# Attention with its work ordered by a build-time model of tasks, and its weighted values in fp32 column halves

## What is computed

```python
x = x + 0.5 * ffn(layernorm(x))                     # experts, top 2 of 8
q = (x @ Wq) -> 16 heads of 64, * 64 ** -0.5        # on layernorm(x)
k, v = split(x @ Wkv)                               # one head each
sim = q @ k.T + rel_bias * 64 ** 0.5; causal mask
x = x + softmax(sim) @ v @ Wout + bout
x = x + 0.5 * ffn(layernorm(x))
```

## Time and profile before

| | |
|---|---|
| median of 3 runs | 1348.94 us (1347.59 to 1349.1) |
| the profiled execution | 1347.8 us, of which the span is 1346.0 us |
| mean granted clock of PE | 0.937 |
| PE, weight loads | busy 1029.9 us (77%), 899.3 (67%) |
| DVE, ACT, POOL | busy 840.0 us (62%), 722.3 (54%), 650.5 (48%) |
| instructions | 23815 |

### The profile page before, as it was taken

One profiled execution on the slowest core, in us unless ns is written; L12 is line 12 of the kernel. 1 busy time (PEld: TensorE's weight loads), 2 busy tenths in 40 slices (PEclk: granted clock), 3 DMA queues, 4 the chain that ended last, 5 costly groups with the idle time before them and its releaser, 6 DMA issues.

```text
span 1346.0 us, 23815 instructions
## 1 busy us (share of the span) xinstructions
PE 1029.9 (77%) x7084; PEld 899.3 (67%) x7084; DVE 840.0 (62%) x2514; ACT 722.3 (54%) x1804; POOL 650.5 (48%) x473
## 2 busy tenths in 40 slices
PE   1428788750899999999999999999999706878870
PEld 1427777740787778878778778877887606777770
DVE  4662222227888887888888888888887493222226
ACT  1102222211888888888889889888898201222220
POOL 1146777743353444434444444444444044777772
PEclk9988999985999999999999999999999658999995
DMA  7896555541000000000000000000000203555545
GB/s 207 116 167 197 147 152 156 151 132 54 1 2 1 1 1 1 2 1 1 1 1 1 1 1 1 1 1 1 1 1 1 63 0 115 154 149 153 152 111 187
DMA packets 61065, 87.13 MB, mean 65 GB/s; under 512 B 8019, under 2 KB 32598, under 8 KB 60944
## 3 DMA queue, kind: packets, MB, share of 16 engines
q1 hardware_dynamic: 51200, 66.08, 18.9%
q0 software_dynamic: 9744, 19.56, 4.9%
HBM read 65.67 MB, written 20.97 MB: 64 GB/s over the span
## 4 chain that ended last, share of the span: by engine, by line
PE 47%; DVE 22%; DMA 10%; issue 9%; POOL 9%; ACT 1%; DVEq 1%; another core or an unknown queue 0%; SPq 0%; POOLq 0%; ACTq 0%
PE bank L1046 8%; DMA xr<-xn_dram,gidx 7%; PE bank L1020 6%; DVE qst L857 6%; PE bank L1036 6%; PE bank L1037 5%; POOL y_dram L504 5%; PE bank L1058 4%; PE bank L1056 4%; DVE prob L879 3%; PE bank L976 3%; POOL xr L498 3%; PE bank L986 3%; DVE x_sb L824 2%; DVE in_tile L753 2%
## 5 line engine op out<-in xcount | busy, mean ns | idle before, releaser
L536 POOL TENSOR_TENSOR prob<-prob,rsum 128x512 f32<-128x512 f32 (+3 forms) x128 | 296.1, 2321 | 381.5 <-DVE rsum L886 381.5
L600 ACT ACTIVATE prob<-prob,negmax 128x384 f32<-128x384 f32 (+3 forms) x512 | 283.2, 556 | 25.9 <-DVE negmax L879 24.2
L879 DVE CUSTOM_DVE_ANT_0 prob<-bank,bias_tab 128x384 f32<-128x384 f32 (+3 forms) x512 | 243.1, 489 | 70.8 <-PE bank L1037 60.2
L578 ACT ACTIVATE hT<-bank 128x512 f32<-128x512 f32 x144 | 86.0, 597 | 372.6 <-PE bank L976 372.6
L891 DVE TENSOR_TENSOR pl<-bank,ph 128x512 fp32r<-128x512 f32 x320 | 219.9, 687 | 26.0 <-ACT ph L609 22.4
L1036 PE MATMUL bank<-kst,qst 128*128 128x256 f32 (+2 forms) x512 | 182.6, 371 | 23.3 <-DVE qst L857 21.0
L609 ACT ACTIVATE ph<-bank 128x512 fp32r<-128x512 f32 x320 | 188.8, 590 | 19.6 <-PE bank L1046 17.3
L1046 PE MATMUL bank<-ident,prob 128*128 128x128 f32 x1280 | 193.7, 274 | 0.7 <-POOL prob L536 0.6
L1046 PEld LDWEIGHTS bank<-ident,prob 128*128 128x128 f32 x1280 | 156.8, 140 | 48.1 <-POOL prob L536 10.2
L815 DVE COPY yo<-bank 128x128 f32<-128x128 f32 x144 | 42.0, 292 | 214.1 <-PE bank L986 209.9
L498 POOL DMA_INDIRECT xr<-xn_dram,gidx x144 | 140.1, 973 | 72.8 <-issue 31.1
(11 more groups left out here) (152 smaller groups left out, 1366.9 us busy)
## 6 DMA issues: line engine op xcount, KB each, us to landing
w1t<-L_ffn_fc_w SPq DMA_DIRECT2D x144, 256.0 KB
in_tile<-y_dram SPq DMA_DIRECT2D x16, 512.0 KB, 4.3
bias_dram<-hg SPq DMA_DIRECT2D x1, 5120.0 KB, 52.9
xn_dram<-in_tile SPq DMA_DIRECT2D x8, 512.0 KB, 2.9
bias_tab<-bias_dram SPq DMA_DIRECT2D x1, 4096.0 KB, 13.0
xr<-xn_dram,gidx POOLq DMA_INDIRECT x144
y_dram<-yo,sidx POOLq DMA_INDIRECT x144
x_sb<-L_attn_x SPq DMA_DIRECT2D x4, 512.0 KB, 7.9
```

The source lines that it names most:

```text
L536: g.tensor_tensor(out=pv, in0=pv, in1=rsum[:, n % 4, :].unsqueeze(2).to_broadcast([P, HG, (n % QT + 1) * P]), op=ALU.mult).then_inc(norm_d ...
L600: a.activation(prob[n % QT][:, h, :], prob[n % QT][:, h, :], ACT.Exp, scale=-1.0, bias=negmax[:, (HG * n + h) % 8:(HG * n + h) % 8 + 1], a ...
L879: v.tensor_tensor_reduce(out=prob[n % QT][:, h, :], in0=front[:, 0:w], in1=bias_tab[:, HG * (n // QT) + h, SEQ - w:SEQ], scale=-1.0, scala ...
```

## The change

Task by task:

- Values are kept in fp32 (`vst`, one ACT copy `VC`, no subtraction). A transposed block is copied once, in fp32, to a ring `pT` of eight blocks, by ACT or by DVE, as the model had it.
- The weighted values of a unit are one task of 2(t + 1) fp32 matmuls of 256 columns with 64 stationary columns: for each block, heads 0 and 2 go to partitions 0 to 63 of the bank, heads 1 and 3 to partitions 64 to 127.
- The copy `ot` has 256 columns, and the output projection two fp32 matmuls that each take two heads at once, with Wout's rows laid out for that and not twice.
- `xTh`, `xTl`, `kst`, `vst` are doubled, `prob` goes from four buffers to eight, `lsum` and `rsum` too.
- The order is made by `attention_order`: it takes all tasks of all batches with a duration, what they need, and which kind of bank they take and free, and plays them through: an engine that is free takes, of the tasks that are ready, the one with the smallest `wanted_at`. Banks are given out in that play, no longer in turn. Semaphore values are counted from the resulting orders.
- The expert stages are the same code.

The core of the diff:

```diff
-RING = 3
+RING = 8
+GROUP = QT * (QT + 1) // 2
+PERIOD = NG * GROUP + 2
+LEAD = 0.7
 S_FIX = 1.1
+HOP = {"same": 0.12, "other": 0.07, "pe": 0.22}
...
-        wo_sb = sb("wo_sb", [P, H, D])
+        wo_sb = sb("wo_sb", [P, NG, 2, D])
...
-            vst = ab("vst", [P, QT, 2 * DH], F32R)
+            vst = ab("vst", [P, 2, QT, DH])
...
-            prob = [ab(f"prob{t}", [P, HG, (t + 1) * P]) for t in range(QT)]
+            prob = [ab(f"prob{n}", [P, HG, (n % QT + 1) * P]) for n in range(8)]
...
-            ph = ab("ph", [P, RING, HG * P], F32R)
-            pl = ab("pl", [P, RING, HG * P], F32R)
-            ot = ab("ot", [P, 2, HG * P])
+            pT = ab("pT", [P, RING, HG * P])
+            ot = ab("ot", [P, 2, 2 * P])
...
+        def attention_tasks():
...
+                    for jj in range(t + 1):
+                        task(("T", b, n, jj), {"pe": 0.44}, [("N", b, n)], "turned")
+                        task(("TC", b, n, jj), {"act": 0.48, "dve": 0.6}, [("T", b, n, jj), ("AV", *ring_user(b, n, jj))],
+                             None, ("T", b, n, jj))
+                    task(("AV", b, n), {"pe": 0.47 * (t + 1) + 0.2}, [("TC", b, n, jj) for jj in range(t + 1)] +
+                         ([("VC", b)] if n == 0 else []) + [("YA", *earlier(b, n, 2))])
...
+        def attention_order():
...
+            while left:
+                for e in order:
+                    if busy[e] > now:
+                        continue
+                    can = [k for k, when in ready[e].items() if when <= now and
+                           (tasks[k][2] is None or any(x[0] <= now for x in free[tasks[k][2]]))]
+                    if not can:
+                        continue
+                    k = min(can, key=wanted_at)
...
+                    order[e].append(k)
+                    left -= 1
+                    busy[e] = now + cost[e]
...
-                        a.activation(ph[:, i % RING, :], PT_BANK[i % 3][:], ACT.Copy).then_inc(ph_done, 1)
+                        a.activation(pT[:, (b * NB + blk(n, jj)) % RING, :], BANK_OF["T", b, n, jj][:], ACT.Copy).then_inc(pt_act, 1)
...
-                        v.tensor_tensor(pl[:, i % RING, :], PT_BANK[i % 3][:], ph[:, i % RING, :].bitcast(F32),
-                                        ALU.subtract).then_inc(pl_done, 1)
+                        v.tensor_copy(pT[:, (b * NB + blk(n, jj)) % RING, :], BANK_OF["T", b, n, jj][:]).then_inc(pt_dve, 1)
...
-                        t_.matmul(OT_BANK[n % 2][:], vst[:, jj, :], ph[:, i % RING, :], start=(jj == 0), stop=False)
-                        pe.wait_ge(pl_done, b * NB + (i + 1))
-                        t_.matmul(OT_BANK[n % 2][:], vst[:, jj, :], pl[:, i % RING, :], start=False, stop=(jj == n % QT)).then_inc(av_ps, 1)
+                        for jj in range(n % QT + 1):
+                            for o in range(2):
+                                heads = pT[:, (b * NB + blk(n, jj)) % RING, :].rearrange("p (c o q) -> p o c q", c=2, o=2)[:, o, :, :]
+                                ins = t_.matmul(BACK_BANK[n % 2][o * DH:(o + 1) * DH, 0:2 * P], vst[:, b % 2, jj, :], heads,
+                                                start=(jj == 0), stop=(jj == n % QT))
+                        ins.then_inc(av_ps, 1)
...
-                        for h in range(HG):
-                            ins = t_.matmul(OT_BANK[n % 2][:, 0:D], ot[:, n % 2, h * P:(h + 1) * P], wo_sb[:, HG * (n // QT) + h, :],
-                                            start=(h == 0), stop=(h == HG - 1))
+                        for c in range(2):
+                            ins = t_.matmul(BACK_BANK[n % 2][:, 2 * P:2 * P + D], ot[:, n % 2, c * P:(c + 1) * P], wo_sb[:, n // QT, c, :],
+                                            start=(c == 0), stop=(c == 1))
```

More of the change, by code:

```diff
@@ L252, in on @@
             return 0 <= k - lag < ETILES
[L254 to L284, removed]
-                a, z = g * group - LEAD + (K_GAP if g == 0 else 0), (g + 1) * group - LEAD
-                for t in range(QT):
-                    for h in range(HG):
-                        done = sum(weight[:t]) + weight[t] * (h + 0.5) / HG
-                        lead(a + (z - a) * done / sum(weight), ("S", 0, g * QT + t, h))
-                    lead(a + (z - a) * sum(weight[:t + 1]) / sum(weight) + LAG_R, ("R", 0, g * QT + t))
-            return sorted(plan, key=lambda x: x[0])
@@ L364, in attention @@
-        def attention(eng, run):
-            run(FIRST, 0)
-            for b in range(BATCH - 1):
-                run(PLAN, b)
-            run(FINAL, BATCH - 1)
+        BACK_BANK = [bank[5], bank[6]]
+        FREE_BANKS = {"front": [bank[0], bank[1], bank[7]], "turned": [bank[2], bank[3], bank[4]]}
         def blk(n, jj):
@@ new lines, in build, with counted @@
+        ORDER, BANK_OF, TAKEN_FROM = attention_order()
+        def counted(engine, kinds, each=1):
+            out, total = {}, 0
+            for k in ORDER[engine]:
+                if k[0] in kinds:
+                    total += each(k) if callable(each) else each
+                    out[k] = total
+            return out
+        MISC_PS, S_PS, PT_PS = counted("pe", ("xT", "K", "V", "Q")), counted("pe", ("S",)), counted("pe", ("T",))
+        AV_PS, PROJ_PS = counted("pe", ("AV",)), counted("pe", ("Y",))
@@ new lines, in build, with freed, in_order @@
+        PLACE = {k: i for e in ORDER for i, k in enumerate(ORDER[e])}
+        def freed(k):
+            if k[0] == "TC":
+                return (pt_act, PT_ACT[k]) if k in PT_ACT else (pt_dve, PT_DVE[k])
+            return {"TTR": (s_done, S_DONE), "VC": (v_done, V_DONE)}.get(k[0], (misc_free, MISC_FREE))[0], \
+                {"TTR": S_DONE, "VC": V_DONE}.get(k[0], MISC_FREE)[k]
+        def in_order(first, second):
+            assert first[1] < 0 or PLACE[first] < PLACE[second], (first, second)
@@ new lines, in build @@
+        for k in ORDER["pe"]:
+            if k[0] == "S":
+                in_order(("T", *earlier(k[1], k[2], 8), k[2] % QT), k)
+            if k[0] == "xT":
+                for reader in (("K", k[1] - 2), ("V", k[1] - 2), ("Q", k[1] - 2, NG - 1, 1)):
+                    in_order(reader, k)
+            if k[0] == "K":
+                for h in range(HG):
+                    in_order(("S", k[1] - 2, NU - 1, h), k)
+            if k[0] == "V":
+                in_order(("AV", k[1] - 2, NU - 1), k)
+            if k[0] == "Q":
+                b2, g2 = (k[1], k[2] - 2) if k[2] >= 2 else (k[1] - 1, k[2] - 2 + NG)
+                for h in range(HG):
+                    in_order(("S", b2, g2 * QT + QT - 1, h), k)
@@ L376, in _ @@
+        for k in ORDER["dve"]:
+            if k[0] == "TTR":
+                in_order(("R", *earlier(k[1], k[2], 8)), k)
         @block.sync
```

475 lines of the change are left out of this document (257 added, 218 removed).

## The result

The changed kernel takes 1259.9 us (median of 4 runs; 1257.9 to 1260.6) against 1348.3 for the kernel before, measured beside it: ratio 0.934, 95% interval 0.932 to 0.935. That is 88 us less, where 64 were forecast.

What follows compares the result with a forecast made beforehand. PE bounds attention with 78.5 us work and 10.0 slack a batch. 78.5 - 7.1 + 2.7 = 74.1, plus 6.5 slack gives 80.6; 7.9 less x 8.12 = 64 us saved, so 1285 us, range 1240 to 1340.

Steps and rivals of the forecast that it cites:

- output projection, 8 passes to 4: Attention, PE: four fp32 matmuls per unit become two, 14.1 to 7.0 us, 7.1 us less a batch.
- a block of values, overlapping: Attention, PE: both column halves' passes run side by side, 0.44 us a block; values cost 2.7 us more a batch overall.
- one pass alone at each unit's end: Attention, PE: halves overlap in turn, so each of 16 units ends with one unpaired pass of 0.22 us.
- rival 2: Attention, PE: going in and out of column halves drains the array, 5.2 us a batch, period 85.8, 1327 us; chance 0.16.
- slack kept: Attention, PE: of 10.0 us slack a batch, about two thirds, 6.5, stays because ACT and DVE get lighter.
- period: Attention, one batch: 80.6 us, which is 7.9 less than before.
- Rival 1: Attention values: column halves run one after the other, period 94.7, 1399 us, or 1428 at the old slack; chance 0.12.
- Rival 3: Attention: fixed order misjudges the chip, late copies hold PE, 1350 to 1365 us, half of it 1320; chance 0.07 beyond 1340.
- Buffers, "they only take waits away": Attention: doubled projection buffers, eight probability buffers and a ring of eight add no instruction; no separate size given.
- values block to block: Sign in PE's timeline of attention: weighted values start 0.44 to 0.5 us from one block to the next.
- bias adds: Sign on POOL in attention: batch-opening bias adds stand 78 to 84 us apart.
- ACT, DVE and the query's wait: Signs in attention: ACT and DVE busy near 63 us a period; PE's waits behind the query's subtraction below 4.7 a batch.

Runs made afterwards that it cites:

- the tuned model: Kernel with values of two neighbouring units together, its order model's durations of scores, projections and values set to traced starts: 1264.7 us, ratio 0.938 to before.
- block by block: Changed kernel with one task of weighted values per block instead of per unit, entering the halves 39.5 times a batch: 1391.7 us on a slower chip, ratio 0.974.
- two units together: Changed kernel with weighted values of two neighbouring units directly behind one another, 8 entries a batch: 1326.8 us on a slower chip, 1254.6 again, ratio 0.929 both.
- old order: Before's order and buffers with the changed kernel's arithmetic (single fp32 copies, column halves block by block, two-matmul projection): 1372.2 us, ratio 1.017 to before.

## Why the prediction came out as it did

The direction, the stage and the bound were right, the measured time lies in the range (1240 to 1340), and 88 us against 64 forecast is a difference of three terms, of which two went one way and the third the other. Per batch:

| step of the prediction | forecast | measured |
|---|---|---|
| output projection, 8 passes to 4 | -7.1 | four passes at 0.11, -7.1 |
| a block of values, overlapping | 0.44 us | 0.43, couples 7 ns apart |
| one pass alone at each unit's end | 3.5 us | none |
| going in and out of halves (rival 2) | 0 in the forecast, 5.2 in the rival | 4.8 (at 0.30) to 5.6 (at 0.35) |
| slack kept | 6.5 of 10.0 | 1.8 |
| period | 80.6 | 77.4 |

74.1 - 3.5 - 0.3 + 5.3 + 1.8 = 77.4. And 3.2 us a batch x 8.12 = 26 us is what separates 1285 from 1260. That the time lies in the range is in part luck: with the pass alone and the slack as measured and nothing for the halves, the sum would have been a period of 72.1 and some 1216 us, under the range's 1240. An unbooked cost of 5.3 us stood against 8.5 us that were booked too high.

*The step that was mis-sized is the slack.* "I keep about two thirds, 6.5, because ACT and DVE go from 74 to 76 of 88 us to about 63 of 80": the reason held only in part. With that relief and before's order the slack stays at 8.3 to 9.5; with the new order and no relief it is 5.9; with both 1.8. So the relief is worth at most 1.7 under the old order and 4.1 under the new one, and the order 4.1 without the relief and 6.5 or more with it: each is worth more where the other is there. The sign was in the earlier trace rows: nearly half of the slack had one cause, a query projection written into the order where its bank is not yet free. That wait stays at 5.6 us a batch with a lighter DVE and is gone with the new order and a full one. I treated a wait that had a name as a share of load.

*The pass left alone* came from the assumption that the halves start in turn. They start in couples; the trace shows this for all 48 units of three batches.

*Rival 2, the cost of going in and out*, came, in the size that it had (0.16 us each way from the length of a transpose less its distance; measured 0.30 to 0.35 for both ways). Whether the array is emptied in that time, as it said, no row shows; the rows show the weight loads that start late. I gave it 0.16 of the chances and left it out of the sum; it should have been in the sum, as a term with a lower bound of 0, and the time of 1327 it gave was wrong because the slack fell and no pass was left alone (4.7 and 3.5 us a batch). The argument I had against it, the change from fp32 to fp32r that costs nothing net, is true and says nothing about halves. My argument for the overlap, that a weight load runs under a matmul, holds inside a group; at its edges the trace shows that it doesn't, and there the price is paid. The Trainium skill, TensorEngine Tiling (Array Packing), Key Properties, says that a change of tiling mode drains TensorE; the traces agree that such a change costs time, with 0.33 us a unit, and show nothing of a drain itself. The Trainium skill's 2.38 times for three column tiles (TensorE: Matmul & The Clock Gate, Part 3, Measured speedup vs the span model) would be 79% of full overlap, an estimate from the page; here two tiles reach all of it inside a unit (0.43 us against 0.86 without halves), and (0.43 x 40) / (0.43 x 40 + 5.3) = 76% with the entries counted.

*Rival 1, halves in sequence*, did not come; what it would have been is near the kernel without halves, whose 87.4 us of work (88.2 in the rival) gave a period of 90.5.

*Rival 3, a misjudged order*, did not come for this order, but the tuned model shows that it can: 2 us a batch from changes in durations of 1 to 3% for scores and projections and of 22% for the projection of the values, with the query's wait back in the trace.

*Buffers, "they only take waits away"*: right, and there was almost nothing to take: 0 for the probabilities, 5 us for the projections. The ring of eight was not tried against one of three.

*The signs that were named*: values block to block took 0.43 us where 0.44 to 0.5 was given, and the bias adds stand 77.4 us apart where 78 to 84 was given, both just outside; ACT, DVE and the query's wait came as given.

What stays open: which of the moves in the new order take which waits, apart from the query's; what the ring has in it; and which of the better durations put the query's projection back where it waits.

## What to carry to other kernels

Split the slack of the bound engine by the names in the waits before you forecast what becomes of it: the wait that one instruction's place in the order made here went only when that place moved, and not with a lighter engine. Relief and order were worth more together than each alone. Count going in and out of column halves as work of TensorE (0.3 us for both here), and put the matmuls of one mode together: blocks by unit instead of singly was worth 7 us in 84, pairs of units another 1. And try a few settings of an order that a model makes, on the chip, before believing that a truer model gives a better one.

## What was unexpected of the hardware

- fp32 matmuls of 64 stationary columns that write the two halves of a bank's partitions run in couples whose two passes start 7 ns apart, at the rate of one: 0.216 us for a couple of 256 columns, with no loss after the second couple of a group.
- The first couple after a full-width matmul starts about 0.09 us late and is followed after 0.27 us instead of 0.216; the next matmul in full width starts 0.10 us late and is followed 0.05 to 0.10 us late. The numbers are the same in five runs (the changed kernel, block by block, two units together on both chips, old order), and in them the first weight load on each side starts with its matmul instead of ahead of it.
- A chip of the same kind took 703 to 711 us for the expert stages of four kernels where the chip of the result took 627, while attention agreed within 0.5%. The cause is open. The 134 against 149 GB/s ahead of attention are the same bytes over a longer time; the packets of the main DMA queue filled 17.2% of 1442 us on one and 20.1% of 1257 on the other, about 250 us on both, so they took no longer. PE's granted clock in that stretch was 0.86 against 0.91.
